# Four diffusion transformer blocks on one core: a new opening, barriers that four engines pass without SyncE, and new places for steps in every stage

## The chip, the cores and the metric

One Trainium2 chip, one of its cores. A run is one launch of the whole program; the metric is the device time of that launch in microseconds. Five instruction streams run side by side: TensorE (PE, matmuls; PEld is its weight load), VectorE (DVE), ScalarE (ACT), GpSimd (POOL) and SyncE (SP), which issues the DMAs.

## The reference, cut to what matters

The input x is 2 x 1024 x 256 float32. Four blocks (layers 0 to 3) are applied one after another, each with self attention, cross attention to 77 context tokens, and an MLP. Ahead of each of the three stands a layer norm that is modulated by numbers made from the conditioning vector. Layer 0:

```
mod = jax.nn.silu(c) @ W_ada + b_ada
sh_msa, sc_msa, sh_x, sc_x, sh_mlp, sc_mlp = jnp.split(mod, 6, axis=-1)
h1 = _modulate(_ln(x), sh_msa, sc_msa)          # x * (1 + scale) + shift
qkv = h1 @ W_qkv + b_qkv
q, k, v = jnp.split(qkv, 3, axis=-1)
x = x + (_attend(_heads(q), _heads(k), _heads(v)) @ W_proj + b_proj)
h2 = _modulate(_ln(x), sh_x, sc_x)
...                                             # cross attention to ctx, added to x
h3 = _modulate(_ln(x), sh_mlp, sc_mlp)
hidden = jax.nn.gelu(h3 @ W_fc1 + b_fc1, approximate=True)
x = x + (hidden @ W_fc2 + b_fc2)
```

The other layers have the same skeleton. Layers 0 and 1 have 16 heads of 16 values ("narrow"), layers 2 and 3 have 16 heads of 64 ("wide"); layer 2 turns queries and keys with rotary tables, and layer 3's MLP is gated. The self attention's softmax needs the maximum of each row of scores.

## The kernel before, in words

The program is written by hand for the five engines. A list called `order` holds steps, such as `("up", S, b, half, m)`, and each engine's program (`tensor_program`, `scalar_program`, `vector_program`, `gpsimd_program`, `sync_program`) walks through the same list and issues its own part of each step. So the list sets the order within each engine, and semaphores (`Signal`, `Waits`) set it between engines: a later step of an engine waits behind an earlier one of the same engine, also where its own inputs are there.

The list is made in stages, numbered 0 to 15: for each layer self attention, the keys and values of the context ("kv"), cross attention, MLP. Stages 0, 4, 8, 12 are the self attentions, 2, 6, 10, 14 the cross attentions, 3, 7, 11, 15 the MLPs. Within a stage a `Plan` collects steps with a place, a number: one unit is one unit of attention (512 queries of four or two heads) or one of the MLP's 32 `up` and `down` steps. `Plan.close` sorts by place. `MOVES` may add an amount to the place of a step; its keys are a stage number and the kind of the step with leading indices. It is empty here.

Between stages that use the same memory for other tiles stands a step `rest`, ten in all: each engine drains, adds to its own semaphore and waits for all five. In the narrow layers self and cross attention share one plan and have no `rest` between them.

What the change touches, in the order of the execution:

- The opening (lines from `first = line[0]`): SyncE loads the conditioning, the columns, the modulation weights of layer 0 (1536 KB), half of x, the first projection weights (768 KB), the other three layers' modulation weights and the rest of x. The step `cond` makes modulation groups of 128 values: four matmuls of two columns on TensorE and an eviction with bias on ScalarE for each group; layer 0 has 12 groups, the layers 1, 2, 3 have 12, 8 and 12. `mods` forms the scale and shift columns from them on VectorE. `ln_stats` and `ln_rstd` make mean and reciprocal root (VectorE, with the square root on ScalarE), `ln_norm` normalizes, `ln_turn` transposes 256 tokens on TensorE and applies the modulation on ScalarE, `ln_split` splits the result in a high and a low part. `w_split` does the same with weights: the high part on VectorE, the low part on GpSimd or VectorE.
- `p16` is a projection of queries or keys in the narrow layers: six matmuls, a first bf16 part by ScalarE, the remainder by VectorE, a second and third bf16 part on GpSimd. `keep16` stores the parts in memory and `stack16` loads them back in the stacked layout.
- `max` makes the row maxima: a matmul into one of the three free PSUM banks of a ring and a reduction on VectorE. `mjoin`, `mturn` bring them into a row, and SyncE copies the row into the stack. Only then `score` and ScalarE's exponential can start.
- `m_load` and `m_split` load and split MLP weights, by chunks through three staging buffers. In the wide layers they stand behind the `rest`, because the memory is taken before. `kv_load` loads the next layer's context weights.
- In the wide cross attention `cs` makes the scores of a unit and their exponential, `cnorm` normalizes the probabilities (reciprocal on VectorE, product on GpSimd), `cturn` transposes them, `cav` multiplies with the values.
- In the wide self attention `begin64` fills parts of the stacks with constants on VectorE, `kstack` and `qstack` copy queries and keys into the stacks (SyncE), `v64` makes the values.

Of the kernel before, what the change touches and what calls it, by code (L numbers as in the profile page):

```python
# [113 lines left out]
MOVES = {}  # L114
# [34 lines left out]
def _build(nc, A, root):  # L149
# [57 lines left out]
    wmod_in = [signal(f"wmod_in{i}") for i in range(4)]  # L207
    mod_out = signal("mod_out")
# [382 lines left out]
    def place_keys(step):  # L591

        kind = [step[0]]
# [23 lines left out]
    def norm_steps(p):  # L617
        out = [("ln_stats", p, t) for t in range(8)] + [("ln_rstd", p)]
# [4 lines left out]
    def norm_put(plan, p, lo, hi):  # L623
# [4 lines left out]
        plan.put(lo + 0.26 * w, 0, [("ln_rstd", p)])  # L628
# [141 lines left out]
    order.append(("identity",))  # L770
    for q in range(4):
        order.append(("ln_turn", first, q))
        if q in (1, 2):
            order.append(("cond", Ls[1], 6 * q - 6, 6 * q))
        order.append(("ln_split", first, q))
        order.extend(("ln_norm", first, t) for t in range(2 * q + 4, min(2 * q + 6, 8)))
    for S in stages:
# [7 lines left out]
        if S.kind in ("self", "cross"):  # L785
# [3 lines left out]
            if L.style == 16:  # L789
# [17 lines left out]
                else:  # L807
# [11 lines left out]
                    if L.i:  # L819
                        plan.put(-9.9, 0, [("ones16", S, 1)])  # L820
# [72 lines left out]
        else:  # L893
# [3 lines left out]
            for b, p in enumerate((S.parts[1], S.parts[1].next)):  # L897
# [6 lines left out]
                if p:  # L904
# [3 lines left out]
                    plan.put(at + 8 * gap, 0, [("ln_rstd", p)])  # L908
# [128 lines left out]
    def tensor_program(e, w):  # L1037
# [14 lines left out]
        for what, *a in order:  # L1052
            if what == "cond":
                L, lo, hi = a
                w.wait_ge(wmod_in[L.i], L.i)
# [306 lines left out]
            elif what == "rest":  # L1362
# [7 lines left out]
                for r in rest:  # L1370
                    w.wait_ge(r, a[0])

# [49 lines left out]
    def scalar_program(e, w):  # L1422
        for what, *a in order:
# [16 lines left out]
            elif what == "ln_turn":  # L1440
# [4 lines left out]
                w.wait_ge(mod_made, (p.L.i, "all"))  # L1445
# [176 lines left out]
    def vector_program(e, w):  # L1622
        for what, *a in order:
# [6 lines left out]
            elif what == "mods":  # L1630
                L, = a
                k, nth = where["cond", L.i, L.nmod - 1]
                w.wait_ge(bank_free[k], nth)
# [834 lines left out]
```

## Time and profile before

| | us |
|---|---|
| median of three runs | 4215.28 |
| lowest and highest | 4209.64, 4217.68 |
| the profiled execution | 4205.3 |
| its span in the trace | 4203.5 |
| TensorE, VectorE, ScalarE, GpSimd busy | 3850.6, 2894.8, 2059.1, 1485.2 |
| mean granted clock of TensorE | 0.962 of full speed |

All places in time below are microseconds from the start of the span. A timeline row gives start, length, engine, line, operation, what it writes and reads, and in brackets how long the engine was idle ahead of it and what released it. Instructions of one kind behind one another are merged in a row.

### The profile page before, as it was taken

To read this page: it belongs to the slowest core of one execution; us is meant where nothing else is said; L and a number is where in the kernel's file an instruction comes from. 1 tells how busy PE (TensorE), PEld (TensorE's weight loads), DVE (VectorE), ACT (ScalarE), POOL (GpSimd) and SP (SyncE) were. 2 spreads that over 40 slices of the span, in tenths; PEclk is the share of its full clock that TensorE was granted. 3 is DMA by queue.
4 is the path that set the end of the run, shared out by engine and by line. 5 is a ranking of instruction groups with operands and counts; after the bars stand their busy time and mean duration, and the time that the engine had idled before them with its cause. 6 is when DMAs were issued, how large, how long until landed. Compare 5 with 4: busy or idle time off the path is not lost. (4 is left out here: it accounts for less than half of the span.)

```text
span 4203.5 us, 53415 instructions
## 1 busy us (share of the span) xinstructions
PE 3850.6 (92%) x19532; PEld 2316.7 (55%) x19532; DVE 2894.8 (69%) x4227; ACT 2059.1 (49%) x3724; POOL 1485.2 (35%) x850
## 2 busy tenths in 40 slices
PE   7999988899998989998999968888999999998989
PEld 6333347533334755545555446666555555546778
DVE  6888755788865667786777735555778777774465
ACT  2666655366665534443444436643444444445641
POOL 2200122220104146665666544421444444451130
PEclk8999989999998989999999989998999999999999
DMA  4233240333323333332332233232332223214320
GB/s 139 42 54 44 46 84 15 61 47 53 40 50 67 81 71 66 67 72 47 71 70 56 44 91 78 63 83 63 70 71 69 57 66 69 63 36 119 91 54 21
DMA packets 151830, 268.10 MB, mean 64 GB/s; under 512 B 33946, under 2 KB 67668, under 8 KB 150544
## 3 DMA queue, kind: packets, MB, share of 16 engines
q1 hardware_dynamic: 151568, 264.67, 29.7%
q8 instruction: 156, 2.56, 0.3%
q14 instruction: 106, 0.87, 0.1%
HBM read 103.96 MB, written 29.64 MB: 32 GB/s over the span
## 5 line engine op out<-in xcount | busy, mean ns | idle before, releaser
L1049 PE MATMUL PS<-t 128*128 128x512 f32 (+4 forms) x7896 | 1951.8, 378 | 108.2 <-DVE t L1705 16.5
L1509 ACT ACTIVATE t<-PS 128x512 f32<-128x512 f32 (+2 forms) x1600 | 1166.4, 750 | 1013.8 <-PE PS L1049 1005.2
L1049 PEld LDWEIGHTS PS<-t 128*128 128x128 f32 (+2 forms) x7896 | 1228.6, 184 | 629.9 <-issue 229.2
L1230 PE MATMUL PS<-t 128*32 128x512 f32 (+2 forms) x4352 | 812.6, 613 | 0.0
L1784 DVE TENSOR_REDUCE t<-PS 128x1 fp32r<-128x1024 f32 x512 | 618.2, 1218 | 238.6 <-PE PS L1121 237.8
L1790 DVE TENSOR_REDUCE t<-PS 128x1 f32<-128x512 f32 x1024 | 645.0, 681 | 58.4 <-PE PS L1125 55.0
L2090 POOL TENSOR_TENSOR t<-t 128x1024 f32<-128x1024 f32 x256 | 620.8, 2425 | 126.4 <-ACT t L1509 102.4
L1121 PE MATMUL PS<-t 128*128 128x512 f32 x1024 | 338.6, 413 | 68.3 <-DVE t L1784 35.8
L2086 POOL TENSOR_TENSOR t<-t 128x1024 f32<-128x1024 f32 x64 | 153.7, 2402 | 679.7 <-PE PS L1240 520.2
L1125 PE MATMUL PS<-t 96*128 96x512 bf16 x1024 | 357.6, 391 | 32.2 <-DVE t L1790 18.7
L1230 PEld LDWEIGHTS PS<-t 128*32 128x32 f32 (+2 forms) x4352 | 170.9, 122 | 328.8 <-issue 326.1
L2003 POOL TENSOR_TENSOR t<-t 128x512 f32<-128x512 f32 x96 | 134.4, 1401 | 551.2 <-DVE t L1682 371.4
L1125 PEld LDWEIGHTS PS<-t 96*128 96x128 bf16 x1024 | 90.7, 97 | 328.0 <-DVE t L1790 139.8
L1121 PEld LDWEIGHTS PS<-t 128*128 128x128 f32 x1024 | 193.2, 195 | 138.6 <-DVE t L1784 53.0
L1272 PE MATMUL PS<-t 128*128 128x256 f32 x1024 | 251.6, 389 | 12.9 <-DVE t L1866 9.1
L1881 DVE TENSOR_TENSOR t<-PS,t 128x1024 f32<-128x1024 f32 x128 | 156.4, 1222 | 130.5 <-PE PS L1272 130.4
L1864 DVE RECIPROCAL PS<-PS 128x256 f32<-128x256 f32 x128 | 224.7, 1755 | 13.3 <-PE PS L1240 13.3
L1272 PEld LDWEIGHTS PS<-t 128*128 128x128 f32 x1024 | 192.2, 193 | 68.8 <-issue 27.7
L1360 PE MATMUL PS<-t 128*128 128x256 f32 x1536 | 215.4, 292 | 7.2 <-POOL t L2096 3.7
L1360 PEld LDWEIGHTS PS<-t 128*128 128x128 f32 x1536 | 203.5, 196 | 19.2 <-issue 5.6
L2077 POOL TENSOR_TENSOR t<-t 128x616 f32<-128x616 f32 x64 | 82.9, 1295 | 335.0 <-DVE t L1835 335.0
L1529 ACT ACTIVATE t<-PS,t 128x77 f32<-128x77 f32 x512 | 159.1, 325 | 82.5 <-DVE t L1826 82.2
(133 smaller groups left out, 3509.3 us busy)
## 6 DMA issues: line engine op xcount, KB each, us to landing
t<-t SPq DMA_DIRECT2D x640, 128.0 KB, 2.6
t<-scr_n SPq DMA_DIRECT2D x288, 128.0 KB, 6.3
t<-t SPq DMA_DIRECT2D x128, 256.0 KB, 3.8
scr_n<-t SPq DMA_DIRECT2D x72, 256.0 KB, 2.4
t<-t SPq DMA_DIRECT2D x256, 64.0 KB, 2.1
t<-in_L_Wg SPq DMA_DIRECT2D x16, 768.0 KB, 4.5
t<-in_L_W SPq DMA_DIRECT2D x36, 256.0 KB, 3.4
t<-in_L_Wo SPq DMA_DIRECT2D x64, 128.0 KB, 2.5
```

The costliest lines, as they stand in the source:

```text
L1049: ins = e.matmul(out, l, r, start=i == 0, stop=i == len(terms) - 1, tile_position=tp)
L1121: ins = e.matmul(o[:, 512 * h:512 * h + 512], u.smq[j][qt], u.smk[j][h], start=True, stop=True)
L1125: e.matmul(o, u.smq[j][qt], u.smk[j][half], start=True, stop=True).then_inc(*bank_full[k].inc(nth))
L1230: ins = e.matmul(banks[S.ot][wd * j:wd * j + wd, :], u.v[j][kt], P[0:S.pr, j, :], start=kt == 0, stop=kt == S.nkt - 1, tile_position=(0, w ...
L1272: ins = e.matmul(o[:, 256 * q:256 * q + 256], S.OR[n % 2][:, 128 * q:128 * q + 128], u.wo[:, :], start=True, stop=True)
L1360: ins = e.matmul(banks[4 + q][:, 0:D], l, r, start=m == 0 and t == 0, stop=m == 7 and t == 2)
L1509: e.activation(dst, src, ACT.Exp, scale=S.L.scale).then_inc(*expd.inc((S.i, i)))
L1529: ins = e.activation(S.PQ[n % 3][:, j, t, :], o[:, 256 * t + CT * b:256 * t + CT * b + CT], ACT.Exp, bias=S.NM[n % 3][:, at], accum_out=S. ...
L1784: e.tensor_reduce(S.MT[m % 2][:, S.nqt * j + qt:S.nqt * j + qt + 1], o, AX.X, ALU.max, negate=True).then_inc(*bank_free[k].nth(nth))
L1790: e.tensor_reduce(S.NMX[m % 2][:, 4 * j + qt, half:half + 1], o, AX.X, ALU.max).then_inc(*bank_free[k].nth(nth))
L1864: e.reciprocal(o[:, hs], o[:, hs]).then_inc(*recip_made.inc((S.i, n, h)))
L2090: e.tensor_tensor(S.AP_[:, :, :], S.AP_[:, :, :], P[1][:, :, :], ALU.add).then_inc(*pool_summed.inc((S.i, n, kt)))
```

## The change

Six things are changed.

1. The opening is rearranged. `mod_load` takes a range of groups: groups 0 to 3 of layer 0 (512 KB) are loaded first, groups 4 to 11 behind the first projection weights. `cond` for these four stands ahead of the statistics. The identity cast and `w_split` stand between the variance and the reciprocal, which is a step of its own (`ln_recip`), and the norms follow. `mods` takes a range of norms and makes only the first one there. Layer 1's groups no longer stand between the transposes: layers 1 and 2 are made at -16.8 in the first plan, the rest of layer 0 and layer 3 in pairs among the first maxima (-9 to -8). Layer 0's weights lie 40 KB further on, under a stack that is filled later.
2. In the first batch of layer 0's self attention the second bf16 part of `p16` is made by VectorE; GpSimd makes only the third.
3. The ones of the second key stack are set by GpSimd later, behind group 11 of layer 0.
4. At a `rest` ScalarE, VectorE and GpSimd wait for four semaphores and TensorE for three (TensorE, ScalarE, VectorE). SyncE waits for all five as before.
5. The signal for modulation is per norm.
6. `MOVES` is filled for stages 0, 3, 4, 7, 8, 10, 11, 12, 14 and 15, some 200 entries.

```diff
-MOVES = {}
+MOVES = {
+    0: {
...
+    3: {
...
+        ('ln_norm', 0, 0): -0.493,
+        ('ln_split', 0, 0): -1.176,
+        ('ln_turn', 0, 0): -0.35,
+        ('max', 'self'): -0.023,
+        ('max', 'self', 0): -0.147,
+        ('p16', 'self'): -0.891,
+        ('p16', 'self', 0): -0.838,
+        ('up', 'mlp'): -0.64,
+        ('up', 'mlp', 1): -0.608,
+    },
...
+    7: {
...
+        ('up', 'mlp'): -1.497,
+        ('up', 'mlp', 0): 0.435,
+        ('up', 'mlp', 1): 0.564,
+    },
+    8: {
...
+        ('max', 'self', 1): -1.09,
...
+        ('score', 'self'): -0.069,
...
+        ('v64', 'self', 1): 0.846,
+        ('wo', 'self'): 1.292,
+    },
...
+    11: {
...
+        ('m_load', 'mlp'): -1.358,
+        ('m_load', 'mlp', 1): 0.079,
+        ('m_split', 'mlp'): -3.199,
...
+        ('up', 'mlp'): -0.894,
...
+    14: {
+        ('begin64', 'cross'): 0.109,
+        ('cav', 'cross'): 0.299,
+        ('cnorm', 'cross'): -0.763,
+        ('cs', 'cross'): -1.421,
...
-        sbt(c, [128, 120])
+        sbt(c, [128, 10360])
...
-    order.append(("ones16", first.stage, 1))
-    order.append(("mod_load", Ls[0]))
+    order.append(("mod_load", Ls[0], 0, 4))
     order.append(("setup", 1))
     order.append(("w_load", first, 0))
-    order.extend(("mod_load", L) for L in Ls[1:])
+    order.append(("mod_load", Ls[0], 4, 12))
+    order.extend(("mod_load", L, 0, L.nmod) for L in Ls[1:])
     order.append(("setup", 2))
+    order.append(("cond", Ls[0], 0, 4))
     order.extend(("ln_stats", first, t) for t in range(8))
-    order.append(("cond", Ls[0], 0, 12))
     order.append(("ln_rstd", first))
+    order.append(("identity",))
+    order.append(("w_split", first, 0, 0))
+    order.append(("mods", Ls[0], 0, 1))
+    order.append(("ln_recip", first))
     order.extend(("ln_norm", first, t) for t in range(4))
-    order.append(("mods", Ls[0]))
-    order.append(("w_split", first, 0, 0))
-    order.append(("identity",))
     for q in range(4):
         order.append(("ln_turn", first, q))
-        if q in (1, 2):
-            order.append(("cond", Ls[1], 6 * q - 6, 6 * q))
...
-                        plan.put(-16.9, 0, [("mods", Ls[1])])
-                        for M, at, then in ((Ls[2], -16.8, -16.6), (Ls[3], -16.74, -16.5)):
-                            plan.put(at, 0, [("cond", M, 0, M.nmod)])
-                            plan.put(then, 0, [("mods", M)])
+                        for M in (Ls[1], Ls[2]):
+                            plan.put(-16.8, 0, [("cond", M, 0, M.nmod)])
+                            plan.put(-16.6, 0, [("mods", M, 0, 3)])
+                        for M, lo, at in ((Ls[0], 4, -9), (Ls[3], 0, -8.667)):
+                            plan.put(at, -8 if lo == 0 else -8.667, [("cond", M, i, i + 2) for i in range(lo, 12, 2)])
+                            plan.put(-7.9, 0, [("mods", M, 1 if lo else 0, 3)])
...
                 e.drain().then_inc(*rest[0].inc(a[0]))
-                for r in rest:
+                for r in rest[:3]:
                     w.wait_ge(r, a[0])
...
+    def leads(S, b):
+        return S.L.i == 0 and not S.after and b == 0
...
+                if leads(S, b):
+                    w.wait_ge(bank_free[k], nth)
+                    e.tensor_copy(S.NAT[:, ch, 3 * qk + 1, ts], r[:, :]).then_inc(*kx_1.inc((S.i, i)))
...
                 e.drain().then_inc(*rest[2].inc(a[0]))
-                for r in rest:
+                for r in rest[:4]:
                     w.wait_ge(r, a[0])
...
-                if S.L.i:
-                    w.wait_ge(v_ones, S.i)
+                w.wait_ge(v_ones, S.i)
+                if not S.L.i:
+                    k, nth = where["cond", 0, 11]
+                    w.wait_ge(bank_full[k], nth)
```

## Rows read from the trace of the kernel before

**Rows 1.** The page, its first part: busy time of the engines.
```profile
PE 3850.6 (92%) x19532; PEld 2316.7 (55%) x19532; DVE 2894.8 (69%) x4227; ACT 2059.1 (49%) x3724; POOL 1485.2 (35%) x850
```
**Rows 2.** Windows: stretch, length, busy time by engine, granted clock, DMA.
```profile
0.00:101.80 101.80, 81.21 (x325) 63.36 (x326) 61.76 (x148) 25.03 (x66) 24.97 (x26) 0.80 0.46 139
...
39.50:75.80 36.30, 33.94 (x155) 31.07 (x153) 20.93 (x61) 12.99 (x31) 17.84 (x20) 0.73 0.61 131
...
101.80:640.00 538.20, 499.19 (x2939) 199.32 (x2938) 421.17 (x808) 338.61 (x388) 93.53 (x93) 0.97 0.33 54
...
2400.00:2500.00 100.00, 65.71 (x275) 41.83 (x275) 38.41 (x46) 34.34 (x86) 46.22 (x27) 0.83 0.29 74
...
3830.00:4030.00 200.00, 190.72 (x1130) 150.72 (x1129) 111.03 (x198) 134.65 (x510) 45.17 (x36) 0.99 0.34 79
```
**Rows 3.** TensorE's waits: line, releaser, us in total, times, longest.
```profile
PE PS L1049 <- DVEq L1987: 8.8, 6, 1.7
...
PE PS L1049 <- SPq L2345: 7.6, 1, 7.6
```
**Rows 4.** Timeline of the opening.
```profile
8.16 10.40 PE L1049 MATMUL PS<-t 128*128 128x2 f32 x48 [8.16 <-DMA t<-in_Wmod]
...
9.61 0.43 DVE L1667 BATCH_NORM_STATS2 t<-t 128x6 f32<-128x256 f32 x1 [4.30 <-DMA t<-in_x]
...
20.16 0.21 ACT L1439 ACTIVATE t<-t 128x8 f32<-128x8 f32 x1
...
22.91 1.02 ACT L1448 ACTIVATE t<-PS,t 128x256 f32<-128x256 f32 x2 [2.53 <-DVE t L1645]
...
23.88 3.42 POOL L2022 TENSOR_TENSOR t<-t 128x1536 fp32r<-128x1536 f32 x1 [19.64 <-DVE t L1705]
23.96 3.62 DVE L1693 CAST t<-t 128x512 fp32r<-128x512 f32 x1
...
29.39 0.43 DVE L1693 CAST t<-t 128x512 fp32r<-128x512 f32 x1 [0.44 <-ACT t L1448]
...
38.72 1.09 PE L1070 MATMUL PS<-t 128*128 128x128 f32 x4
```
**Rows 5.** Timeline: a projection step on GpSimd, and VectorE at the first maxima.
```profile
47.54 0.61 POOL L2043 CAST t<-t 128x512 bf16<-128x512 f32 x1
...
48.23 1.16 POOL L2045 TENSOR_TENSOR t<-t 128x512 bf16<-128x512 f32 x1
...
76.47 19.22 DVE L1790 TENSOR_REDUCE t<-PS 128x1 f32<-128x512 f32 x32
```
**Rows 6.** Timeline: start of layer 2's self attention, of SyncE, VectorE and TensorE.
```profile
1499.79 5.30 SPq L2247 DMA_DIRECT2D t<-t  x8
...
1505.77 1.57 DVE L1723 MEMSET t<- 64x512 f32 x3 [6.17 <-SPq L2345]
...
1514.33 4.64 DVE L1784 TENSOR_REDUCE t<-PS 128x1 fp32r<-128x1024 f32 x4
...
1532.09 0.96 DVE L1705 CAST t<-t 128x1536 fp32r<-128x1536 f32 x1 [7.28 <-DMA t<-in_L_Wg]
...
1536.10 2.35 PE L1121 MATMUL PS<-t 128*128 128x512 f32 x4 [5.60 <-DVE t L1784]
```
**Rows 7.** Timeline of TensorE in layer 0's MLP.
```profile
754.43 5.65 PE L1049 MATMUL PS<-t 128*128 128x512 f32 x24
...
774.14 2.31 PE L1125 MATMUL PS<-t 96*128 96x512 bf16 x5 [7.03 <-DMA t<-scr_n]
```
**Rows 8.** Timeline at the start of layer 2's MLP.
```profile
2758.71 0.43 DVE L1960 CAST t<-t 128x512 fp32r<-128x512 f32 x1 [8.68 <-DMA t<-in_L_W]
...
2760.91 2.93 PE L1360 MATMUL PS<-t 128*128 128x256 f32 x12 [3.70 <-POOL t L2096]
```
**Rows 9.** Timeline at the start of layer 3's cross attention.
```profile
3811.77 1.99 PE L1152 MATMUL PS<-t 128*77 128x128 f32 x8 [3.43 <-POOL t L2077]
```
**Rows 10.** Timeline at the second batch of layer 2's self attention.
```profile
1968.27 1.22 PE L1121 MATMUL PS<-t 128*128 128x512 f32 x2 [11.99 <-DMA t<-t]
```

More of the change, by code:

```diff
@@ L207, in _build @@
     wmod_in = [signal(f"wmod_in{i}") for i in range(4)]
+    wmod_first = signal("wmod_first")
     mod_out = signal("mod_out")
@@ L591, in place_keys @@
     def place_keys(step):
-        kind = [step[0]]
+        kind = ["ln_rstd" if step[0] == "ln_recip" else step[0]]
         at = []
@@ L617, in norm_steps @@
     def norm_steps(p):
-        out = [("ln_stats", p, t) for t in range(8)] + [("ln_rstd", p)]
+        out = [("ln_stats", p, t) for t in range(8)] + [("ln_rstd", p), ("ln_recip", p)]
         for q in range(4):
@@ L627, in norm_put @@
             plan.put(lo + 0.03 * w * t, 0, [("ln_stats", p, t)])
-        plan.put(lo + 0.26 * w, 0, [("ln_rstd", p)])
+        plan.put(lo + 0.26 * w, lo + 0.26 * w, [("ln_rstd", p), ("ln_recip", p)])
         at, pace = lo + 0.3 * w, 0.7 * w / 4.9
@@ L1054, in tensor_program @@
                 L, lo, hi = a
-                w.wait_ge(wmod_in[L.i], L.i)
+                w.wait_ge(wmod_first if L.i == 0 and hi == 4 else wmod_in[L.i], L.i)
                 w.wait_ge(silu_done, 0)
@@ L1444, in scalar_program @@
                     w.wait_ge(ln_split[on_pool(was)], (was.i, q - 1 if q else 3))
-                w.wait_ge(mod_made, (p.L.i, "all"))
+                w.wait_ge(mod_made, (p.L.i, p.s, "all"))
                 o, k, nth = full(w, ("ln", p.i, q))
@@ L1630, in vector_program @@
             elif what == "mods":
-                L, = a
-                k, nth = where["cond", L.i, L.nmod - 1]
-                w.wait_ge(bank_free[k], nth)
-                k, nth = where["cond", L.i, L.nmod - 2]
-                w.wait_ge(bank_free[k], nth)
-                k, nth = where["cond", L.i, L.nmod - 3]
-                w.wait_ge(bank_free[k], nth)
+                L, lo, hi = a
+                last = L.nmod if hi == 3 else 4
+                for m in range(last - 3, last):
+                    k, nth = where["cond", L.i, m]
+                    w.wait_ge(bank_free[k], nth)
                 mod = mods[L.i]
-                for s, (sh, sc, aff) in enumerate(L.norms):
+                for s in range(lo, hi):
+                    sh, sc, aff = L.norms[s]
                     for k in range(2):
@@ L1644, in vector_program @@
                         if aff is None:
-                            e.tensor_copy(mb, mod[:, 2 * sh + k, :]).then_inc(*mod_made.inc((L.i, "all")))
+                            e.tensor_copy(mb, mod[:, 2 * sh + k, :]).then_inc(*mod_made.inc((L.i, s, "all")))
                         else:
@@ L1650, in vector_program @@
                             w.wait_ge(mod_made, (L.i, s, k, 1))
-                            e.tensor_scalar(ma, ma, col(aff + "_w", k), None, ALU.mult).then_inc(*mod_made.inc((L.i, "all")))
+                            e.tensor_scalar(ma, ma, col(aff + "_w", k), None, ALU.mult).then_inc(*mod_made.inc((L.i, s, "all")))
             elif what == "ln_stats":
@@ L1673, in vector_program @@
                 e.tensor_scalar(ln_sd[:, :], ln_mv[:, :, 1], p.L.eps, None, ALU.add).then_inc(*ln_var.inc(p.i))
+            elif what == "ln_recip":
+                p, = a
                 w.wait_ge(ln_root, p.i)
@@ L1987, in vector_program @@
                 e.drain().then_inc(*rest[2].inc(a[0]))
-                for r in rest:
+                for r in rest[:4]:
                     w.wait_ge(r, a[0])
@@ L2042, in gpsimd_program @@
                     w.wait_ge(nat_kept[ch], (S.i, 0) if b else (S.after.i, 1))
-                e.tensor_copy(S.NAT[:, ch, 3 * qk + 1, ts], S.NR2[i % 2][:, :]).then_inc(*nat_1.inc((S.i, i)))
-                w.wait_ge(nat_1, (S.i, i))
+                if leads(S, b):
+                    w.wait_ge(kx_1, (S.i, i))
+                else:
+                    e.tensor_copy(S.NAT[:, ch, 3 * qk + 1, ts], S.NR2[i % 2][:, :]).then_inc(*nat_1.inc((S.i, i)))
+                    w.wait_ge(nat_1, (S.i, i))
                 e.tensor_tensor(S.NAT[:, ch, 3 * qk + 2, ts], S.NR2[i % 2][:, :], S.NAT[:, ch, 3 * qk + 1, ts],
@@ L2098, in gpsimd_program @@
                 e.drain().then_inc(*rest[3].inc(a[0]))
-                for r in rest:
+                for r in rest[:4]:
                     w.wait_ge(r, a[0])
@@ L2123, in sync_program @@
             elif what == "mod_load":
-                L, = a
-                e.dma_start(Wmod[L.i][:, :, :], A[f"Wmod{L.i}"]).then_inc(*wmod_in[L.i].inc(L.i, 16))
+                L, lo, hi = a
+                ms = slice(128 * lo, 128 * hi)
+                e.dma_start(Wmod[L.i][:, :, ms], A[f"Wmod{L.i}"][:, :, ms]).then_inc(*(wmod_first if hi < L.nmod else wmod_in[L.i]).inc(L.i, 16))
             elif what == "ln_bias":
@@ L2168, in sync_program @@
                     for qk in range(S.nqk):
-                        w.wait_ge((nat_0, nat_1, nat_2)[part],
+                        w.wait_ge((nat_0, kx_1 if leads(S, b) else nat_1, nat_2)[part],
                                   (S.i, b, ch, 1, qk) if part == 0 else (S.i, p16_index(S, b, ch, 1, qk)))
```

171 lines of the change are left out of this document (168 added, 3 removed).

## The prediction

> **What bounds the kernel now.** I read the page first: TensorE is busy for 3850.6 of 4203.5 us, so at most 353 us can come from its idle time [rows 1]. Next the windows by stage: long attention stretches run at a granted clock of 0.97 to 0.99 with little idle time, the first 101.8 us hold 20.6 us of idle at 0.80, and the 100 us at the start of layer 2's cross attention hold 34 us of idle at 0.83 [rows 2]. So the time is matmul work, and what an edit of order can touch lies at the opening and at stage starts. Third, TensorE's waits by releaser: SyncE at a barrier stands there once, with 7.6 us [rows 3]. Last the timelines at the stage starts, where a single wait of 3 to 12 us stands ahead of each [rows 4, 6 to 10].
>
> Durations are of the profiled execution, 4205.3 us with a span of 4203.5. It lies 10 us under the median of 4215.28; I form the difference in the trace and subtract it from either.
>
> **Opening, up to the start of the projections.** Now the 12 modulation groups of layer 0 run one after another, 48 matmuls in 10.40 us or 0.87 us a group, from 8.16 us, when the 1536 KB arrive. The square root stands behind them and ends at 20.37, although the statistics (eight pairs of 0.53 us from 9.61) end near 13.9. Reciprocal, norms and transposes follow, and the first normalized quarter is taken from PSUM at 22.91 [rows 4]. After the change 512 KB come first. The next 512 KB (x) arrived 1.45 us behind the weights (9.61 against 8.16), so 1024 KB less ahead of x is about 2.8 us: statistics from 6.8 instead of 9.61, ended at 11.1. Four groups (3.5 us) end by about 9.5. The root ended 1.8 us after the last group's matmuls (20.37 against 18.56), most of it table load; it ends by 11.7 if the load precedes the wait for the variance, by 12.9 if not. Behind the variance VectorE now issues the identity cast (0.21), the high part of the first weights (0.95; 768 KB that should be in by 10.6 at the same rate), four small modulation instructions (0.3), then the reciprocal: 13.1. But the high part releases GpSimd's low part, 3.42 us, and in the trace a VectorE cast begun beside it took 3.62 us, against 0.43 for the same shape at 29.39 [rows 4]. I let the first norms wait for it too: 16.1. Two norms, four transposes (1.1) and ScalarE (1.02) and the two splits (0.43 and 0.7) then give a first split ended at about 20.1; before, its cast alone ended at 27.6.
>
> This is where the Trainium skill speaks against the new order ("SBUF — State Buffer", section "Who interferes with whom"): the shared port pair is an exclusive lock, a VectorE `tensor_scalar` or cast in a two-port mode can need it, and the loser waits for the whole instruction. The 3.62 us row agrees for the cast; whether the norm is caught in the opening no run here shows. By the rule the sum stands as I have it; without it the opening would gain 3 us more.
>
> The other quarters then follow at 2.3 us (1.02 on ScalarE, 0.43 and about 0.7 on VectorE, handoffs), because layer 1's 12 groups no longer stand between the transposes. The last transposes come near 24 instead of 38.72, and the projections, right behind them, start 15 us earlier. Bounds: 12, if weights or root come late; 18, if GpSimd blocks nothing.
>
> **Projections to first score.** From 39.5 to 75.8 TensorE was busy 33.9 of 36.3 us [rows 2]: 8 projections, 20 groups (layers 2 and 3), 4 values. After, it is 8, 20 (layers 1 and 2), 4: nothing gained. In 8 projection steps the bf16 cast goes from GpSimd to VectorE. GpSimd's step is 0.61 and 1.16 us at a pitch of 1.80 [rows 5]. A VectorE cast (0.43) ahead of 1.16 with two handoffs gives about 1.8 if the two exclude each other; if not, it could fall towards 1.4, the time of a projection's six 512-column matmuls (24 took 5.65 us [rows 7]). I take 0; bounds 3 us of gain and 1 of loss. The ones memset had nobody behind it at GpSimd's head; in its new place it can hold only GpSimd's bias steps, and x needs its bias only at the first output projection.
>
> Then the first maxima: 32 reductions of 0.60 us, 19.22 us on VectorE with nothing beside them. Now 20 groups (8 of layer 0, 12 of layer 3, in pairs) stand among them, in the same ring of three banks. TensorE needs 20 x 0.87 = 17.4 us for the groups and, at 0.2 to 0.4 us for each 512-column bf16 maximum, 6 to 13 for the maxima: 24 to 30 us. I take 27: 8 us longer than now. Bounds: 5 and 17 (no overlap at all). The modulation of layer 3 and the rest of layer 0 (about 20 of VectorE's smallest instructions) lies beside the copy of the maxima. Opening net: 15 - 8 = **7 us**; ends 13 and -5.
>
> **Barriers.** Four engines no longer wait for SyncE; SyncE still waits for all, so no load behind a barrier starts sooner. TensorE waited for SyncE once, 7.6 us; six times the barrier was released by VectorE's own queue [rows 3]: nothing there. At the one of layer 1's MLP VectorE stood idle for 6.17 us until 1505.77, so it had ended at 1499.6; SyncE was issuing the query stack until 1505.1 [rows 6]. Now the memsets begin near 1500. They take 8.6 us (1505.77 to 1514.33), then the first maximum can be reduced: 1508.6, and the query stack, whose issue does not move, should have landed by then. So 5.7 us, less about 1 because the earlier `up` steps of that MLP push the rotary chain back by up to one 1.4 us group (a step of (a) without its `down`). I take **5 us**; ends 0 and 6.
>
> **Places.** Four of the new places meet a stall that the trace shows.
> (a) MLP of layer 0: projections of the next attention's first half move 1.73 steps ahead, its norm 0.35 to 1.18. TensorE stood 7.03 us for the stacked keys [rows 7]. A step is about 2.8 us there (six 512-column matmuls, 1.4, and twelve of half the columns), but the `up` steps move 1.25 too: 3 us; ends 0 and 7.
> (b) Start of layer 2's self attention: maxima of unit 1 move 1.09 units ahead, past the split of weight group 1, for whose DMA VectorE stood 7.28 us while TensorE stood 5.60 [rows 6]. 5 us; ends 0 and 7.
> (c) MLP of layer 2: weight loads move 1.36 ahead of the step at which three context loads stand. Now these are issued ahead of the third weight chunk; VectorE stood 8.68 us for it, and TensorE 3.70 [rows 8]. 4 us; ends 0 and 5. The wait before the first chunk stays.
> (d) Layer 3's cross attention: scores 1.42 units ahead, reciprocals 0.76. TensorE stood 3.43 us for the first normalized probabilities [rows 9]; scores of units 1 and 2 now fill it. 4 us; ends 0 and, with the 9.3 us that the steady part idles [rows 2], 10.
> Unchanged stay the 12 us at layer 2's second batch [rows 10] and most of the idle time at its cross attention: the new places there leave the order of the first steps. All other places (mostly hundredths of a unit, in loops that run at 0.97 to 0.99) I take at 0; the idle time of such a loop, 39 us in layer 0's self attention [rows 2], lets me bound them all at 20 either way.
>
> Sum: 7 + 5 + 3 + 5 + 4 + 4 = **28 us**. The execution of 4205.3 would take 4177; the median 4215.3 - 28 = **4187 us**.
>
> **Rivals.**
> A. *Only opening and barrier pay*: the re-placed steps give in one loop what they take in another. 7 + 5 = 12: 4203. For it: unnamed moves are many and touch loops whose idle time is a few tenths of a microsecond at a time. Against: (b) and (c) change who stands behind a DMA wait.
> B. *More than forecast*: the waits for VectorE in the loops shrink as well, and stalls at the low clock cost double: 28 + 25 = 53: 4162. For it: the lowest clocks [rows 2] lie where the stalls are. Against: nothing shows that hundredths of a unit reorder a loop for the better.
> C. *Slower, by the bank ring of layer 3's cross attention.* Scores 1.42 units ahead stand directly behind the transposes of three units before, and each unit takes four of three double banks. If TensorE then stood in each of 31 units for half of the first unit's 3.43 us, that is 53 us; with 24 gained elsewhere the result is 29 slower: 4244. It decides from 24/31 = 0.8 us a unit on. Against: now TensorE idles 9.3 us there in all [rows 2].
> D. *The opening gives its gain back*: groups among the maxima do not overlap (17 us) and the head gains 12: -5. The rest gives 21, so 16: 4199.
>
> **Chances.** Forecast 0.40, A 0.22, B 0.16, C 0.07, D 0.10, and 0.05 that nothing moves. A measurement of this kernel tells about 0.2% (8.4 us) from none. Faster by over 0.2%: forecast, B, nearly all of D, four fifths of A: 0.83. Within: 0.10. Slower: C: 0.07. The range runs from just under B to the edge of no change: 4158 to 4212; outside it lie C, part of the still case and a little beyond B.
>
> **What would show it.** First exponential at about 95 instead of 101.76; projections from 25; ScalarE's root under 13; no TensorE wait for SyncE's drain, and layer 2's first maximum reduced near 9 us after the barrier; the waits of 7.03, 5.60, 3.70 and 3.43 us gone or halved; the DMA wait at layer 2's second batch still near 12. The forecast is wrong in its steps if the maxima of unit 0 take under 22 or over 32 us, if the first norm does not wait for GpSimd, or if a steady loop (windows of equal work) changes by over 5 us either way.

## The result, and the profile after

The changed kernel took 4186.9 us (median of 4 runs, 4173.8 to 4188.3), the kernel before 4213.0 beside it on the same chip (4209.6 to 4217.7). The ratio worked out from all executions is 0.9928, 95% interval 0.9911 to 0.9946: faster by 0.5 to 0.9%. (The quotient of the two medians by themselves would be 0.9938.) The profiled execution took 4186.25 us with a span of 4184.3, 19.2 less than the span before.

The first part of the page of the changed kernel, as [rows 1]:

```profile
PE 3861.7 (92%) x19532; PEld 2307.5 (55%) x19532; DVE 2886.0 (69%) x4235; ACT 2047.3 (49%) x3724; POOL 1470.4 (35%) x842
```

Span less busy time was 352.9 us and is 322.6: 30.3 us of idle time are gone. Busy time grew by 11.1 us with the same 19532 matmuls, so idle time was partly traded for longer matmuls: by the table below, matmuls ran for 235 us at the lower clock level before and for 255 now. The table splits this by stage. It is worked out from the matmul records and the clock records of one execution of each kernel, a stage ending with its last matmul, the first beginning 1.9 us into the span: length, time without a running matmul, and time of running matmuls at the lower of the clock's two levels, in us. Of each stage the first is before, the second has the new opening and barriers but no new place, the third is the change.

```
              before              no new place        after
L0 attention  662.0  63.4  72.1   656.7  61.7  82.7   653.0  60.3  75.2
L0 MLP        138.8  19.7   8.6   139.3  20.6   7.9   136.5  16.8   6.8
L1 attention  568.1  43.0  34.3   571.1  46.3  32.3   572.4  42.4  42.0
L1 MLP        127.8   7.1   6.1   126.2   7.0   2.8   128.6   7.8   5.8
L2 self       939.3  69.6  30.0   934.8  63.2  33.8   940.5  63.9  41.1
L2 cross      305.2  56.6  17.2   307.8  56.7  22.6   312.1  57.0  35.3
L2 MLP        135.7  13.7  11.5   135.5  14.6   9.2   128.1   9.0   5.2
L3 self       904.6  42.0  30.3   903.4  41.9  27.5   896.8  32.8  23.7
L3 cross      263.4  20.8  19.7   261.5  20.8  15.6   258.2  16.2  15.6
L3 MLP        147.0   7.3   5.2   146.8   7.0   5.4   146.6   7.3   4.3
```

Timeline of the changed kernel's opening, against [rows 4]: start and length in us, queue, line, operation, tiles, count, in brackets the idle time before it and what ended it.

```profile
6.12 3.57 PE L1249 MATMUL PS<-t 128*128 128x2 f32 x16 [6.12 <-DMA t<-in_Wmod]
7.59 0.43 DVE L1869 BATCH_NORM_STATS2 t<-t 128x6 f32<-128x256 f32 x1 [2.28 <-DMA t<-in_x]
12.17 0.21 ACT L1642 ACTIVATE t<-t 128x8 f32<-128x8 f32 x1 [0.88 <-DVE t L1875]
13.12 0.16 DVE L1847 COPY t<-t 128x2 f32<-128x2 f32 x1
13.22 3.43 POOL L2229 TENSOR_TENSOR t<-t 128x1536 fp32r<-128x1536 f32 x1 [12.77 <-DVE t L1909]
13.26 3.41 DVE L1847 COPY t<-t 128x2 f32<-128x2 f32 x1
16.59 0.19 DVE L1879 RECIPROCAL t<-t 128x8 f32<-128x8 f32 x1
18.83 1.02 ACT L1651 ACTIVATE t<-PS,t 128x256 f32<-128x256 f32 x2 [6.45 <-PE PS L1270]
23.98 1.12 PE L1270 MATMUL PS<-t 128*128 128x128 f32 x4 [1.13 <-DVE t L1886]
24.75 2.06 PE L1249 MATMUL PS<-t 128*128 128x512 f32 x4
```

Every forecast point but one holds within 1 us: four groups until 9.69, the root before 13, VectorE held until GpSimd's 3.43 us end (16.65), last transposes at 23.98, projections at 24.75. The one that does not is the reciprocal, forecast for 13.1 and started at 16.59. It was not the norm that GpSimd held: the second of two copies of 128x2 elements took 3.41 us where the first took 0.16, and reciprocal and norms stand behind it.

The same kernel's first maxima, on VectorE, against [rows 5], and the first exponential on ScalarE:

```profile
59.61 0.68 DVE L1997 TENSOR_REDUCE t<-PS 128x1 f32<-128x512 f32 x1
82.91 2.48 DVE L1997 TENSOR_REDUCE t<-PS 128x1 f32<-128x512 f32 x4 [1.21 <-PE PS L1325]
86.61 2.48 DVE L1997 TENSOR_REDUCE t<-PS 128x1 f32<-128x512 f32 x4 [1.21 <-PE PS L1325]
90.30 0.69 DVE L1997 TENSOR_REDUCE t<-PS 128x1 f32<-128x512 f32 x1 [1.21 <-PE PS L1325]
91.92 0.16 DVE L1844 TENSOR_SCALAR t<-t 128x2 f32<-128x2 f32 x1
93.64 0.20 DVE L2024 COPY t<-PS 16x128 bf16<-16x128 bf16 x1
98.55 1.02 ACT L1712 ACTIVATE t<-PS 128x1024 f32<-128x1024 f32 x1 [7.14 <-PE PS L1249]
```

The reductions start 16.9 us earlier than [rows 5], then take 31.4 us instead of 19.2. The copy of the row of maxima on VectorE starts 2.65 us behind the last reduction, behind the modulation from 91.92 on, where it started 0.69 behind it before; from there to the exponential it is 0.5 us less than before. So 16.9 - 12.2 - 2.0 + 0.5 = 3.2: the first exponential is at 98.55 instead of 101.76.

Start of layer 2's self attention (barrier, second weight group), against [rows 6]:

```profile
1494.50 4.43 PE L1249 MATMUL PS<-t 128*128 128x256 f32 x24 [1.75 <-DVEq L2194]
1494.63 1.57 DVE L1927 MEMSET t<- 64x512 f32 x3 [0.43 <-DVEq L2194]
1495.98 11.12 SPq L2460 DMA_DIRECT2D t<-t  x16
1502.78 2.08 PE L1321 MATMUL PS<-t 128*128 128x512 f32 x4 [3.85 <-DMA t<-t]
1504.04 2.36 DVE L1991 TENSOR_REDUCE t<-PS 128x1 fp32r<-128x1024 f32 x2 [0.87 <-PE PS L1321]
1526.48 0.95 DVE L1909 CAST t<-t 128x1536 fp32r<-128x1536 f32 x1
1527.64 9.66 PE L1249 MATMUL PS<-t 128*128 128x512 f32 x30
```

TensorE waits 1.75 us at the barrier, the first maximum is reduced 9.5 us after it (forecast: near 9), and what is late next is the query stack's own DMA, 3.85 us. At the weight split both waits of 7.28 and 5.60 us are gone.

Against [rows 7, 8, 9, 10]: the stacked keys in layer 0's MLP, the weight loads of layer 2's MLP, the first units of layer 3's cross attention, and layer 2's second batch.

```profile
765.40 0.82 PE L1325 MATMUL PS<-t 96*128 96x512 bf16 x3 [1.91 <-DMA t<-scr_n]
...
2746.39 11.96 SPq L2548 DMA_DIRECT2D t<-in_L_W  x8
2751.78 8.21 PE L1249 MATMUL PS<-t 128*128 128x512 f32 x24 [6.90 <-POOL t L2308]
2756.11 0.52 DVE L2167 CAST t<-t 128x512 fp32r<-128x512 f32 x1 [1.12 <-DMA t<-in_L_W]
2758.40 0.43 SPq L2465 DMA_DIRECT2D t<-in_ctxT  x1
...
3803.74 1.08 PE L1364 MATMUL PS<-t 77*64 77x512 f32 x4 [1.77 <-ACT t L1740]
...
1956.38 1.22 PE L1321 MATMUL PS<-t 128*128 128x512 f32 x2 [11.96 <-DMA t<-t]
```

The 7.03 us are 1.91, the 3.70 us between layer 2's MLP steps are gone (the wait of 6.90 ahead of its first chunk stays, as said), GpSimd's 3.43 us is a wait of 1.77 for ScalarE, and the 12 us at the second batch stand as they stood.

### The profile page after: what moved, and what is told of

It is laid out like the page before. It is cut to its first block, busy times and chain, and to the rows that moved or that the text cites. A ratio compares the mean times of both kernels' runs of the same rounds, so it can differ in the third digit from the quotient of the medians.

```text
span 4184.3 us, 53400 instructions
## 1 busy us (share of the span) xinstructions
PE 3861.7 (92%) x19532; PEld 2307.5 (55%) x19532; DVE 2886.0 (69%) x4235; ACT 2047.3 (49%) x3724; POOL 1470.4 (35%) x842
## 4 chain that ended last, share of the span: by engine, by line
PE 46%; DVE 6%; POOL 4%; issue 3%; SPq 2%; ACT 2%; DMA 1%; POOLq 0%; DVEq 0%; ACTq 0%
PE PS L1249 22%; PE PS L1430 9%; PE PS L1472 5%; PE PS L1321 4%; PE PS L1560 2%; DVE t L1991 2%; POOL t L2302 1%; PE PS L1440 1%; PE PS L1352 1%; DVE PS L2071 1%; PE PS L1364 1%; POOL t L2275 1%; SPq L2460 1%; SPq L2443 1%; POOL t L2283 1%
## 5 line engine op out<-in xcount | busy, mean ns | idle before, releaser
L1249 PE MATMUL PS<-t 128*128 128x512 f32 (+5 forms) x7896 | 1956.7, 379 | 109.1 <-DVE t L1909 16.5
L1712 ACT ACTIVATE t<-PS 128x512 f32<-128x512 f32 (+2 forms) x1600 | 1154.5, 750 | 1008.4 <-PE PS L1249 1002.4
L1249 PEld LDWEIGHTS PS<-t 128*128 128x128 f32 (+3 forms) x7896 | 1222.4, 183 | 656.4 <-issue 249.5
L1321 PE MATMUL PS<-t 128*128 128x512 f32 x1024 | 337.8, 413 | 47.3 <-DVE t L1991 20.6
```

The costliest lines, as they stand in the source:

```text
L1249: ins = e.matmul(out, l, r, start=i == 0, stop=i == len(terms) - 1, tile_position=tp)
L1321: ins = e.matmul(o[:, 512 * h:512 * h + 512], u.smq[j][qt], u.smk[j][h], start=True, stop=True)
L1712: e.activation(dst, src, ACT.Exp, scale=S.L.scale).then_inc(*expd.inc((S.i, i)))
```

## Experiments

Times are medians with the kernel before beside them on the same chip; different experiments ran on different chips, and what is compared between them are the ratios. 0.001 of a ratio is 4.2 us, and the intervals reach 3.5 to 7.5 us either way. Executions of one kernel differ by up to 19 us, so idle times in the traces carry the finer verdicts.

**The opening alone.** The changed kernel with empty MOVES and the old barriers:

```diff
-    for r in rest[:3]:      (rest[:4] on the other engines)
+    for r in rest:
-MOVES = { ... }
+MOVES = {}
```

> The changed kernel with an empty MOVES and the old barriers, so the new opening (and the cast moved to VectorE) alone. Forecast as put: 7 us under the kernel before. Theory from the changed trace, where the first exponential stands 3.0 us earlier (98.8 against 101.8) although the first maximum stands 17 us earlier: 3 us, with the whole difference in place at the first exponential. Rival D (the opening gives its gain back): 0 or slower. First maximum reduced at 59.6, the 32 maxima over in 31 to 32 us.

4205.5 us, 0.9996 (0.9988 to 1.0005): between 5 us of gain and 2 of loss. The first exponential is at 96.7, 5.1 us earlier than before. VectorE and ScalarE there, and the window up to it as in [rows 2]:

```profile
91.22 0.21 DVE L1826 COPY t<-PS 16x128 bf16<-16x128 bf16 x1 [0.36 <-PE PS L1185]
...
96.66 2.11 ACT L1514 ACTIVATE t<-PS 128x1024 f32<-128x1024 f32 x2 [5.70 <-PE PS L1051]
```

```profile
0.00:96.70 96.70, 75.33 (x325) 59.45 (x326) 62.80 (x156) 25.31 (x66) 20.51 (x18) 0.75 0.49 146
```

Two things differ from the reading above. The copy of the row of maxima, at 91.22, starts 0.69 us behind the end of the last reduction, as in the kernel before, with the modulation behind it. So what holds this copy in the changed kernel is not the opening but one of the new places, `('mturn', 'self', 0): 0.528` of stage 0, which puts it behind the modulation at -7.9 (in the kernel before with the same places the copy starts 1.93 us behind the last reduction instead of 0.69); the six kernels with the new opening and without the places of stage 0 have the first exponential at 96.1 to 97.7, the two with them and the opening as it stands at 98.55 and 99.58. And the 5 us are not idle time: up to the first exponential TensorE is idle for 21.4 us here and for 20.6 before, and busy for 75.3 us instead of 81.2.

The gain is still there when layer 0's attention ends: that stage takes 653 to 661 us in those six kernels, 662 and 665 in the two with the old opening and no places, with the same idle time. Behind it, in the execution profiled here, layer 1's attention is 3.4 us and layer 2's cross attention 6 us longer than before, with hardly more idle time (1.6 more and 1.1 less). Whether the gain reaches the end the time does not tell.

**The barriers alone.** The kernel before with the shorter lists of waits:

> The kernel before with the new barriers alone. Theory: 5 us (0 to 6), all of it at the barrier into layer 2's self attention, where VectorE's memsets begin near 1500 and the first maximum is reduced about 5.7 us earlier. Rival: nothing, because the weights or stacks that SyncE issues are late next and the gain is lost by the next stage.

4204.0 us, 0.9991 (0.9982 to 0.9999): 0 to 8 us. The trace shows the barrier that was named: VectorE's memsets begin at 1508.61 behind its own queue, not SyncE's.

```profile
1508.34 5.31 SPq L2247 DMA_DIRECT2D t<-t  x8
1508.48 3.11 PE L1049 MATMUL PS<-t 128*128 128x256 f32 x24 [1.75 <-DVEq L1987]
1508.61 1.57 DVE L1723 MEMSET t<- 64x512 f32 x3 [0.43 <-DVEq L1987]
```

Layer 2's self attention takes 934.6 us instead of 939.3, with 4.9 us less idle time; no other stage lost more than 1 us of idle time by it.

**Both, without new places.** The change with MOVES empty:

> The changed kernel with an empty MOVES: opening and barriers. Forecast 12 us under the kernel before; from the changed trace 8 (3 and 5). If the parts add up, it is the sum of the first two kernels of this call, and what it lacks to the changed kernel's 26 us is the sum of the places. Rival A has it at the changed kernel's time.

4199.9 us, 0.9980 (0.9971 to 0.9988), so 5 to 12 us for opening and barriers together, where the two alone gave 2 and 4 by their ratios. **And the places without them**, the kernel before with the new MOVES:

> The kernel before with the filled MOVES alone. Forecast: 16 us (a to d), with waits of 7.03, 5.60, 3.70 and 3.43 us gone or halved. Rival A: nothing in sum. From the changed trace: the places give in layer 2's MLP (7), layer 3's self attention (8) and cross attention (5) and take in layer 1's self attention (4) and layer 2's cross attention (7).

4190.1 us, 0.9956 (0.9942 to 0.9970): 13 to 24 us. The halves, 8.4 and 18.5, add to 27 where the whole has 30 by its ratio: they add within their intervals. Two thirds of the gain are the places'.

**Only the four named places.** The change with MOVES cut to what the prediction priced:

```diff
+MOVES = {3: {p16, ln_norm, ln_split, ln_turn as in the change},
+         8: {('max', 'self', 1): -1.09},
+         11: {('m_load', 'mlp'): -1.358, ('m_load', 'mlp', 1): 0.079},
+         14: {('cs', 'cross'): -1.421, ('cnorm', 'cross'): -0.763}}
```

> The changed kernel with only the four named places in MOVES: (a) projections and norm in stage 3, (b) maxima of unit 1 in stage 8, (c) weight loads in stage 11, (d) scores and reciprocals in stage 14. Forecast: 16 us under the kernel with an empty MOVES (4199.9), so about 4184. Rival: the named places remove their waits and little else; the rest of the gain comes from places that the prediction left at 0, among them layer 3's self attention, where TensorE idles 42 us with the empty MOVES and 33 with the full one: then 4190 or more, with layer 3's self attention still at 903 us and its idle time at 42.

4197.2 us, 0.9971 (0.9959 to 0.9983). Against the kernel without places that is 4 us by the ratios and 2.7 by the medians, not 16; the two intervals overlap, and together they leave room from 2 us of loss to 10 of gain. By stage: (a) layer 0's MLP 139.3 to 135.7, idle time 20.6 to 16.5; (b) layer 2's self attention 934.8 to 929.1, but idle time only 63.2 to 61.4, in part because 2.9 us in waits of 0.4 to 0.65 us stand where one of 5.46 and one of 0.65 stood; the rest is less time at the lower clock level; (c) layer 2's MLP 138.3, where the kernels without its places have 135.5 to 137.5, so nothing gained; (d) layer 3's cross attention 261.5 to 262.7, idle time 20.8 to 20.5: two waits for ScalarE, 0.91 and 1.49 us, came with the new order. For (c) the timeline of this kernel shows what took the place of the wait:

```profile
2737.29 16.75 SPq L2353 DMA_DIRECT2D t<-in_L_W  x8
2754.08 0.43 SPq L2270 DMA_DIRECT2D t<-in_ctxT  x1
2763.05 2.40 PE L1054 MATMUL PS<-t 96*128 96x154 f32 x8 [5.38 <-issue]
```

Eight weight loads occupy SyncE's queue for 16.75 us, because a load is issued only when its buffer has been split, and the context loads stand behind them, first issued at 2754.08. The context projections (96x154) then start 9 us later, after 5.38 us without work on TensorE. The profile names no releaser for this wait; that it is these loads is read from the order of the queue.

**Loads and splits.** The partner that (c) lacked: MOVES holds only the weight loads and `('m_split', 'mlp'): -3.199`.

> New opening and new barriers, and of the places only the weight loads (1.36 ahead) and the weight splits (3.2 ahead) of layer 2's MLP. With the loads alone TensorE's wait of 3.7 to 4.9 us went and one of over 5 came behind the late context loads: stage 138.3 against 135.5. If the splits are what was missing, the stage falls under 133 us and the time by 2 to 6 from 4199.9. If the steps of the MLP's matmuls have to move too (0.9 and 1.2 ahead), it stays at 135 to 139 us.

4197.3 us, 0.9975 (0.9967 to 0.9984). The stage takes 131.5 us instead of 135.5, its idle time falls from 14.6 to 11.8. So loads and splits together pay; with the steps of the matmuls moved as well the changed kernel has 128.1 and 9.0. That is about 4 us for the pair, 7 for the stage's whole set, nothing for the loads alone. The splits alone were not run, so what the loads add to them is not shown, and the whole time (its interval overlaps that of the kernel without places) does not tell the 4 us.

**One stage of small places.** The largest fall of idle time stood where I had forecast none, in layer 3's self attention. MOVES holds that stage's 15 entries:

> New opening and new barriers, and of the new places only those of layer 3's self attention (15 entries; all but one are under 0.25 of a unit). Theory (small places in a steady loop pay): its idle time falls from 41.9 to about 33 us, the kernel is 8 to 10 us faster than without any place (4199.9), near 4191. Rival, that of the prediction (hundredths of a unit do nothing by themselves, the gain there came from what the stages ahead left behind): idle time stays at 41 to 42 and the time at 4200.

4191.0 us, 0.9962 (0.9951 to 0.9973): 7.6 us under the kernel without places by the ratios, 8.9 by the medians. Idle time in the stage falls from 41.9 to 31.4; all six kernels without its places have 41.5 to 42.1. **And one of the 15**, all scores of that stage 0.07 of a unit ahead:

```diff
+MOVES = {12: {('score', 'self'): -0.07}}
```

> As the kernel with only the places of layer 3's self attention, but with one entry of the 15: scores 0.07 of a unit ahead. If this reordering of score matmuls behind the averaging matmuls of the unit before is what pays, the idle time of that stage falls by 5 us or more, and the time to about 4194. If it is the single places (values of the second half 1.32 units ahead and others), the idle time stays within 2 us of 41.9 and the time near 4200.

4194.7 us, 0.9967 (0.9954 to 0.9980): 5.5 us by the ratios, 5.2 by the medians, with intervals that overlap; the idle time of 34.5 is the finer verdict: 7.4 of the 10.5 us come from this entry. TensorE's waits in that stage (line, releaser, us in total, times, longest), first without places, then with this entry:

```profile
PE PS L1123 <- DVE t L1793: 16.6, 8, 4.9
PE PS L1123 <- DMA t<-t: 9.1, 9, 1.3
```

```profile
PE PS L1123 <- DVE t L1793: 14.0, 9, 4.0
PE PS L1123 <- DMA t<-t: 2.6, 5, 1.2
```

L1123 makes the maxima's scores. What fell most are its nine short waits for a DMA. Where the order differs, the pair of score matmuls at the end of a run of 16 now stands ahead of the group of 24 matmuls of 256 columns and not behind it. That this is how the waits go is my reading of the order; no run isolates it further.

**Without the places of layer 2.** MOVES without its stages 8 and 10 (self and cross attention of layer 2):

> The changed kernel without the places of stages 8 and 10 (layer 2's self and cross attention). From the traces: with them layer 2's self attention takes 940.5 us against 934.8, with the wait of 5.5 us gone but as much idle time as before, and the cross attention 312.1 against 305 to 311. Theory (these places take in the loop what they give at its start, and more): 5 to 10 us faster than the changed kernel, the 5.5 us wait back. Rival (the differences are the low clock of single executions): no difference.

4173.1 us, 0.9917 (0.9903 to 0.9930). Span less busy time is the same (324 us and 323 in the changed kernel), and matmuls at the lower clock fall from 255 to 225 us. Not all of this belongs to the edit: 14 of the 30 us lie in layer 1's attention, whose order is the same in both kernels. The stretch that shows it, 50 us of equal work in layer 2's cross attention (length, busy times of TensorE, weight loads, VectorE, ScalarE and GpSimd, granted clock, DMA share, GB/s), first of the changed kernel and with two parts of it, then without these places:

```profile
2531.00:2581.00 50.00, 40.82 (x215) 31.89 (x216) 30.13 (x59) 31.07 (x105) 26.13 (x18) 0.86 0.23 56
2546.00:2551.00 5.00, 3.27 (x16) 3.27 (x17) 2.59 (x7) 2.53 (x6) 2.00 (x2) 0.50 0.53 120
2556.00:2561.00 5.00, 4.18 (x13) 3.56 (x13) 3.39 (x5) 1.30 (x3) 1.99 (x2) 0.50 0.66 143
```

```profile
2519.00:2569.00 50.00, 41.01 (x230) 31.01 (x229) 32.62 (x60) 32.36 (x106) 27.17 (x20) 0.97 0.23 56
2539.00:2544.00 5.00, 4.59 (x25) 3.69 (x24) 3.91 (x6) 4.07 (x12) 3.73 (x3) 0.74 0.00 0
```

And the two waits in this stretch, in the timeline of TensorE, first of the changed kernel:

```profile
2547.73 1.11 PE L1270 MATMUL PS<-t 128*128 128x128 f32 x4 [3.90 <-DVE t L1886]
2556.82 1.12 PE L1270 MATMUL PS<-t 128*128 128x128 f32 x4 [2.78 <-DVE t L1886]
```

```profile
2537.64 0.66 PE L1079 MATMUL PS<-t 128*128 128x128 f32 x4 [4.28 <-DVE t L1695]
...
2545.82 0.66 PE L1079 MATMUL PS<-t 128*128 128x128 f32 x4 [1.82 <-DVE t L1695]
```

In the changed kernel TensorE waits twice for a norm on VectorE, 3.90 us until 2547.73 and 2.78 until 2556.82, and the clock in the rows of 2546 and 2556 is 0.50, the 1.2 GHz level. Without the places the same two waits are 4.28 and 1.82 us, and the clock falls once, behind the first (0.92 and 0.74 in the rows of 2534 and 2539). The sum of the waits differs by 0.6 us, the stage by 4 (312.1 against 308.2). This repeats. The four profiled kernels with these places all have waits of 3.90 and 2.8 to 2.9 us, with the clock at the lower level for 13.7 us around and behind them, and 312.1 to 313.0 us in this stage; the ten others have 4.3 and at most 1.8 us, with 3.4 or 6.8 us of it, and 305.2 to 311.3 us. In the self attention, too, the three kernels with the new barriers and all places of stage 8 take 4 to 8 us longer than the five without any. Which of the two stages brings how much of the whole time was not run. By the whole time the gain is not secured: the intervals of 0.9917 and 0.9928 overlap.

**The groups in one block.** To price the 20 groups among the maxima, all are put ahead of the first maximum:

```diff
-    plan.put(at, -8 if lo == 0 else -8.667, [("cond", M, i, i + 2) for i in range(lo, 12, 2)])
+    plan.put(-9.05, -9.05, [("cond", M, i, i + 2) for i in range(lo, 12, 2)])
```

> The changed kernel with the 20 modulation groups in one block ahead of the first maxima. Among the maxima they took 31.5 us together, against 19.2 for the maxima alone, so the overlap hid some 5 of 17 us. Theory: maxima back at 19 to 20 us, first exponential 5 us later than 98.8, kernel 5 us slower. Rival (pairs and maxima in one ring of three banks hinder each other so that nothing is hidden): first exponential within 1 us.

4183.5 us, 0.9951 (0.9938 to 0.9965); the interval overlaps that of the changed kernel, so the time gives no price. On VectorE:

```profile
60.03 0.42 DVE L1953 TENSOR_TENSOR t<-PS,t 128x256 f32<-128x256 f32 x1 [0.62 <-PE PS L1249]
74.76 19.23 DVE L1997 TENSOR_REDUCE t<-PS 128x1 f32<-128x512 f32 x32 [14.30 <-PE PS L1325]
```

The block costs VectorE 14.30 us in one piece. Among the maxima the ten pairs make gaps of 0.59 to 1.21, and the 32 reductions take 12.2 us longer than by themselves. Interleaving hid 2.1 us of the 14.3, and the first exponential comes at 101.22 instead of 98.55 (99.58 in the other kernel with the same opening).

**The low part of the first weights on VectorE**, so that GpSimd is silent while the reciprocal is due:

```diff
-    order.append(("w_split", first, 0, 0))
+    order.append(("w_split", first, 0, 1))
...                                             (two waits for this split follow it)
```

> The changed kernel with the low part of the first weights made by VectorE (two instructions of 0.96) in place of GpSimd's one of 3.43. In the changed trace a copy of 128x2 took 3.41 us beside it. Theory (VectorE was shut out while GpSimd ran): every small copy takes 0.16, the reciprocal starts near 15.1 instead of 16.59 and the first quarter is taken from PSUM 1.4 us earlier than 18.83. Rival (the copy waited for something else): the 3.4 us copy stays and the reciprocal comes 1.9 us later.

One execution: 4185.4 us. Timeline:

```profile
13.64 1.83 DVE L1913 TENSOR_TENSOR t<-t 128x768 fp32r<-128x768 f32 x2
15.45 0.16 DVE L1847 COPY t<-t 128x2 f32<-128x2 f32 x1
15.59 0.16 DVE L1847 COPY t<-t 128x2 f32<-128x2 f32 x1
15.66 0.19 DVE L1879 RECIPROCAL t<-t 128x8 f32<-128x8 f32 x1
```

The copies take 0.16 us again, the reciprocal comes 0.93 us earlier although the 1.83 us of the low part stand ahead of it, and the first exponential is at 96.7 instead of 98.55, of which up to 1 us can be the difference between executions. What held the copy was GpSimd's instruction.

**Three of these together**: this cast, of stage 8 only `('max', 'self', 1): -1.09`, and no stage 10.

> The changed kernel with three edits: the low part of the first projection weights is cast by VectorE, of the places of layer 2's self attention only the maxima of unit 1 are kept (1.09 units ahead), and the places of layer 2's cross attention are left out. Theory (effects of separate parts add): leaving out the places of both stages gave about 10 us (4173 for the kernel without them), the one place kept gives 5.7 more (its stage fell from 934.8 to 929.1 when it stood alone), and the cast about 1.5: near 4166, ratio to the kernel before 0.990. Rival (the places and the stretches at the low clock do not add): within 3 us of the kernel without stages 8 and 10, 4170 to 4176.

4169.9 us, 0.9912 (0.9900 to 0.9925): the lowest ratio measured here, 17 us under the changed kernel's median and 7 by the ratios, with overlapping intervals. The profiled execution has 312 us of idle time (span less busy) against 323 in the changed kernel. Against the kernel without stages 8 and 10 it is 3 us faster where the sum said 7, and the intervals overlap: the time neither bears the sum out nor refutes it. The place kept for (b) takes 3.2 us of idle time and 3.0 of length off its stage here, not 5.7.

## Why the prediction was right, and where it was not

The time was right (4187 forecast, 4186.9 measured), with the forecast sum of 28 us against 30 by the ratio and 26 by the medians. The sum came out by compensation, though, which is luck: the named places gave 4 us where 16 were forecast, and the others, put at nothing, gave what was missing.

1. *What bounds it.* Right for the whole: 30.3 us of idle time went, none of the matmuls. Wrong for the opening, where the 5.1 us came out of TensorE's busy time (81.2 to 75.3 us) and none out of its idle time.
2. *Opening up to the projections, 15 us.* Right: 14.7 (last transposes 38.72 to 23.98), with one step out of place. A copy that took 0.16 us by itself took 3.41 beside GpSimd's 3.43, and 0.16 again with GpSimd silent. The Trainium skill ("SBUF — State Buffer", section "Who interferes with whom") says that the loser waits for the whole instruction; the trace agrees. The copy was the victim, not the norm, which made the reciprocal 3.5 us late (16.59 for 13.1); since the norms stand behind both, the sum is the same.
3. *First maxima with 20 groups in 27 us.* Mis-sized: 31.4 (30.4 in the kernel with the opening alone). The forecast took more overlap for granted than there is: 12.2 us longer against 8. From projections to maxima 2.1 us were gained, inside the bounds of 3 and -1. Net 5.1 at the first exponential for the opening by itself instead of 7, and 2 (-2 to 5) in its time. In the changed kernel it is 3.2, because a place of stage 0 puts the row of maxima behind the modulation; that belongs to item 6.
4. *Barriers, 5 us.* Right: 4.7 in the stage that was named, no idle time at the others. The limit after it was mis-read: the query stack's DMA ends TensorE's wait, where I had the stack landed.
5. *Named places, 16 us.* Wrong: 4 by the ratios. (a) was right, 3.6 for 3. (b) was over-sized: the stage was 5.7 us shorter once and 3.0 once, but its idle time fell by 1.8 and 3.2, since part of the wait of 5.60 came back as short ones; in the full set the other 21 entries of stage 8 give it back (940.5). (c) was wrong by what stood behind it on the same queue: "these are issued ahead of the third weight chunk" was turned into a gain without asking what the context loads feed; by the order of the queue the wait moved to them (5.38 us). (d) was wrong: the 3.43 us wait went and the idle time of the stage did not, until other entries of its set moved too (20.8 to 16.2).
6. *All other places, 0.* This is the step that failed most, and the one whose own test ("if a steady loop changes by over 5 us") it fails: layer 3's self attention fell by 7.8 us, and one entry of 0.07 of a unit takes 7.4 us of idle time off that stage by itself. "Mostly hundredths of a unit" was read as no change of order; in a loop it moves a matmul pair past another in each unit where the two were near. All places together take 26.6 us of idle time (349.2 to 322.6), the four named ones 4.2; those in layer 2's two attentions give some back through the clock, and one of stage 0 costs 2 us at the first exponential. The bound of 20 either way did hold it.
7. *The 12 us at the second batch, and layer 2's cross attention, stay.* Right for idle time (11.96; 56.6 to 57.0). The stage became 7 us longer all the same, by the clock.

Of the rivals, A (opening and barriers alone pay) is refuted by the places' 13 to 24 us in the kernel before. D (the opening ends 5 us behind, 4199 in all) is refuted: its interval ends at 2 us of loss, and the first exponential comes 5.1 us earlier. C's bank ring did not bite: layer 3's cross attention is 5.2 us shorter. B's mechanism, waits that shrink in loops, is shown for layer 3's self attention, with about 8 of its 25 us.

What stays open: how much of the opening's 5 us reaches the end; whether the weight splits of layer 2's MLP would pay without the loads; which entries of stages 8 and 10 bring the longer second wait for the norm; and by what way the entry of 0.07 shortens its waits.

## What to carry to other kernels

Price a moved load together with what frees its buffer and with what stands behind it on its queue: alone it gained nothing here, and a stall appeared at another consumer. In an order laid out by position, a shift of hundredths is a change wherever two steps lie that near, so compare the two orders line by line in each loop before calling it nothing. And look at the clock behind a stall: a stage with the same idle time was 4 us longer where one of two waits, 0.4 us shorter than without the places, and the other, 1.0 us longer, were each followed by matmuls at the lower level. Last, look at where each new place puts a step that others wait for: one entry of stage 0 put the copy of the row of maxima 2 us later, and took back two of the five that the new opening had gained.

## What was not expected of the hardware

- An instruction as small as 128x2 elements on VectorE (0.16 us) took 3.41 us beside a GpSimd instruction of 3.43 that began 0.04 us before it.
- Executions of one kernel with the same order differ by up to 19 us (the one with layer 3's self attention places alone from 4184.3 to 4203.1), with the mean granted clock between 0.965 and 0.959; the slowest is among those with the lowest.
- Groups of matmuls of two columns hardly hide among others: 20 groups cost VectorE 12.2 us spread over ten gaps against 14.3 us in one.
